# Two ends of a sorted edge list by turns: a new chunk order and one-hots summed on GpSimd in a graph kernel

## The chip, the cores and the metric

One core of a Trainium2 chip runs the whole kernel. The metric is the device time of one execution in microseconds, from the chip's own clock, as the median of several runs. The profile shows one execution: TensorE (PE, with its weight loads as PEld), VectorE (DVE), ScalarE (ACT), GpSimd (POOL), the DMA queues (SPq, ACTq) and the TensorE clock that was granted.

## What is computed

There are N = 12,500 nodes with D = 128 features and E = 200,000 edges. The edges are sorted by their target node `dst`. A target is drawn as 12500·u², so low nodes have very many edges and high nodes few. Each edge has 128 features for layer 1 and 64 for layer 0.

```python
# layer 0
h = relu(layernorm(x))
agg = segment_sum(edge_attr_64 @ W_edge.T, dst)
degree = clip(segment_sum(ones, dst), 1)
out_neigh = (agg / degree) @ W_neigh.T
x = x + concat([h @ W_self.T, out_neigh]) @ W_final.T + b_final
# layer 1
h = relu(layernorm(x))
agg = segment_sum(edge_attr_128, dst)
x = x + relu(concat([h, agg]) @ W1 + b1) @ W2 + b2
```

The two sums over edges and the degrees are nearly all of the memory traffic and most of the matmuls. All of it is float32.

## The kernel before

**Chunks.** The edge list is cut into CH = 128 chunks in order. Chunks 0 to 31 hold 13 units of 128 edges, the others 12, and the last one 7. A chunk is made of 1, 2, 3 or 4 batches (`PARTS`, by quarter of the list). The targets of one batch all lie within a window of WIN = 64 nodes that begins at the batch's first target.

**Sums of a chunk** (`sums`, L447). VectorE builds one-hot rows of every unit in float32 (`one_hots`, L821, one instruction at L817 for a whole chunk, three chunks ahead). TensorE multiplies edge features with them. The array is used as two halves of 64 output rows. L462 and L464 sum the two halves of the 128 features side by side. Then, for two units at a time, L479 sums the 64 features of one unit into one half and those of another into the other, and L482 multiplies a block of ones (bfloat16) with the same one-hots, which gives the degrees. A float32 matmul is issued as two instructions, a bfloat16 one as one. All of it lands in one of three PSUM banks. VectorE adds every batch's window into the running sums `agg` in SBUF at the place that a table of bases gives (`adds`, L842, instruction at L856, one for each batch).

**Order.** The chunks run in the order of the list, so the sums of the nodes become final in the order of the nodes. `agg` is one ring of eight groups of 512 nodes plus a pad of 64 columns, cleared by GpSimd (L357, L383) and folded by VectorE (`fold`, L912). NG = 25 groups of four node tiles (two in the last) are taken when their chunks are through. `READY[g]` says after which chunk. It is 26 for the first group and 119, 122, 125, 127, 128 for the last five, since late chunks hold few edges for each node.

**Ticks.** Every engine's program is one list, written by hand in ticks `t`, one for each chunk and 13 more. Behind the chunk of tick t each engine gets the stages of groups that are due: TensorE's `neigh` at READY (L514, L515), `turn` at +6 (L493), `hidden` at +8 (L526, L527) and `output` at +10 (L534). VectorE has `layer_0` at +1, `stats_2` at +2, `scale_2` at +4 and `result` at +11. GpSimd has `add_b2` at +6 (L378) and `clear` at +9. ScalarE has the rest and the store. A group's own part (layer norm, `turn` and `own_part` at L502, `add_b0` L365 and `add_self` L372 on GpSimd) hangs on no edge and is laid out by `SELF`. It begins at tick 2 and comes every 1.6 ticks up to tick 41.

**Slack between the engines.** Loads run five slots ahead (`load_edges` waits for the sums five chunks back), one-hots three chunks ahead, and `sums(t)` waits for the adds of chunk t-3. `neigh` waits for the adds of the chunk just before.

**Start.** The targets of the list are turned into tables by quarters: `relative` (L805, VectorE), `table` (TensorE, L414), `copy_table` (VectorE). At tick t VectorE has `relative(t + 1)` behind `adds(t)` and `one_hots(t + 3)`, and TensorE has `table(t)` one tick later. `check` (VectorE, tick 6) verifies that every target lies in its window and in the part of the ring that is clear.

Of the kernel before, what the change touches and what calls it, by code (L numbers as in the profile page):

```python
# [14 lines left out]
P = 128  # L15
# [14 lines left out]
RING = 8 * GW  # L30
# [8 lines left out]


def chunk_of(e):
    return int(e // (13 * P)) if e < 32 * 13 * P else int(32 + (e - 32 * 13 * P) // (12 * P))
# [12 lines left out]
def build_gnn(nc, x, dst, edge_attr_128, edge_attr_64, W_self, W_neigh, W_edge, W_final, b_final,  # L55
# [6 lines left out]
    NG = -(-N // GW)  # L62
# [4 lines left out]
    def ready(g):  # L67
        t = GW * (g + 1)
        if t >= N:
            return CH  # L70
        s = (t / N) ** 0.5
        t += 11 * N * s * (s * (1 - s) / E) ** 0.5 + 12
        return min(CH, chunk_of((t / N) ** 0.5 * E) + 1) if t < N else CH

    READY = [ready(g) for g in range(NG)]
    FOLDS = [g for g in range(8, NG, 8)]


    SELF = []
    for g in range(NG):  # L80
        t = max(2 + (8 * g) // 5, SELF[-1] + 1 if g else 0)
        while any(t + 4 == r + 6 or t + 6 == r + 10 for r in READY):
            t += 1
        SELF.append(t)
    TICKS = CH + 13
    assert all(b - a >= 1 for a, b in zip(READY, READY[1:]))
    assert all(SELF[g] + 8 < READY[g] + 1 for g in range(NG))

    def tiles_of(g):
        return min(GN, NT - g * GN)  # L90


    def clear_of(c):
        e = first_edge(c + 1) if c + 1 < CH else E
        return min(NG, int((N * (e / E) ** 2 + WIN + 130) // GW) + 1)

    CLEAR = [max(min(8, c), clear_of(c)) for c in range(CH)]
    for c in range(CH):
        assert CLEAR[c] <= 1 or CLEAR[c] <= min(8, c) or READY[CLEAR[c] - 9] + 9 < c
    ADDED = [0]  # L100
    for c in range(CH):
        ADDED.append(ADDED[-1] + len(batches_of(c)))


    tp_use, row_use = {}, {}
    for t in range(TICKS):
        for g in range(NG):
            if t == READY[g] + 6:
                tp_use["n", g] = len(tp_use)
            if t == READY[g] + 10:  # L110
                row_use["n", g] = len(row_use)
        for g in range(NG):
            if t == SELF[g] + 4:
                tp_use["s", g] = len(tp_use)
            if t == SELF[g] + 6:
                row_use["s", g] = len(row_use)
    assert len(tp_use) == len(row_use) == 2 * NG

    SLOTS = 5
# [3 lines left out]
    X_SEMS = 8  # L123
    WARM_UP = 16
# [6 lines left out]
    PASSES = GW // WIN  # L131

    with ExitStack() as ctx:
# [5 lines left out]

        agg = sb("agg", [P, 3, RING + WIN])  # L140
        x0 = sb("x0", [P, NG, GN, D])
        ring128 = sb("ring128", [P, SLOTS, UNITS, D])
        ring64 = sb("ring64", [P, SLOTS, UNITS, D64])
        onehot = sb("onehot", [P, HOTS, UNITS, WIN])
        rel = sb("rel", [P, 4, UNITS, 32])
        base = sb("base", [1, CH, 4], I16)
        base_pair = base[0:1, :, :].rearrange("p c b -> p (c b)").bitcast(I32)
# [20 lines left out]
        steps_lo = sb("steps_lo", [P, NG])  # L168
        steps_hi = sb("steps_hi", [P, NG])
# [19 lines left out]
        FIRST_SCRATCH = 17  # L189
        flat = x0[:, :, :, :].rearrange("p g t f -> p (g t f)")  # L190
        at = [FIRST_SCRATCH * GW]

        def scratch(cols):
            at[0] += cols
            assert at[0] <= (NG - 2) * GW
            return flat[:, at[0] - cols:at[0]]
# [25 lines left out]
        s_xpad, s_hot, s_mm, s_added, s_zero = (sem(n) for n in ("s_xpad", "s_hot", "s_mm", "s_added", "s_zero"))  # L222
# [26 lines left out]
        def every_group(eng, group):  # L249
            with eng.Fori(0, NG - 1) as g:  # L250
                group(g)
            group(NG - 1)
# [6 lines left out]
        def _(sp):  # L259
# [4 lines left out]
            def load_edges(c):  # L264
                slot, e0, R = c % SLOTS, first_edge(c), run_of(c)
                if c >= SLOTS:
                    sp.wait_ge(s_mm, c - SLOTS + 1)
# [16 lines left out]
            sp.wait_ge(s_store, 16 * (NG + 1))  # L284

            def general():
                sp.dma_start(gen_dst_i, dst.rearrange("(p e) -> p e", p=GP)).then_inc(s_gdst, 16)

                def group(g):
# [7 lines left out]
                    if not isinstance(g, int):  # L297
                        rows = x[bass.ds(g * GW, GW), :].rearrange("(j p) f -> p j f", p=P)
                        sp.dma_start(x0[:, 0, 0:2, :], rows[:, 0:2, :]).then_inc(s_gx, 16)
                        sp.dma_start(x0[:, 0, 2:4, :], rows[:, 2:4, :]).then_inc(s_gx, 16)  # L300
                        sp.wait_ge(s_gstep, g * GSTEPS + GSTEPS + 1)
                        rows = out[bass.ds(g * GW, GW), :].rearrange("(j p) f -> p j f", p=P)
                        sp.dma_start(rows[:, 0:2, :], x0[:, 0, 0:2, :]).then_inc(s_gst, 16)
                        sp.dma_start(rows[:, 2:4, :], x0[:, 0, 2:4, :]).then_inc(s_gst, 16)
                    else:
                        n0 = g * GW
                        sp.dma_start(x0[:, 0, 0, :], x[n0:n0 + P, :]).then_inc(s_gx, 16)
                        sp.dma_start(x0[0:LAST_N, 0, 1, :], x[n0 + P:N, :]).then_inc(s_gx, 16)
                        sp.wait_ge(s_gstep, g * GSTEPS + GSTEPS + 1)
                        sp.dma_start(out[n0:n0 + P, :], x0[:, 0, 0, :]).then_inc(s_gst, 16)  # L310
# [9 lines left out]
        def _(pool):  # L320
# [796 lines left out]
```

## Time and profile before

| | |
|---|---|
| median of 3 runs | 602.6 us (598.23 to 602.62) |
| the profiled execution | 595.72 us, its span 593.9 us |
| PE busy | 539.3 us (91%) |
| PEld busy | 485.2 us (82%) |
| DVE busy | 367.4 us (62%) |
| ACT busy | 150.6 us (25%) |
| POOL busy | 134.7 us (23%) |
| DMA | 169.67 MB, mean 286 GB/s |
| chain that ended last | PE 82%, issue 6%, DVE 5%, ACT 4% |

A busy time is the union of an engine's instructions. PE's idle time over the whole span is 593.9 - 539.3 = 54.6 us. "issue" in a list of waits means that the engine waited for nothing that the profile shows.

### The profile page before, as it was taken

How to read it: one execution, taken by the hardware profiler on the slowest of the kernel's cores; microseconds unless marked ns; L12 is line 12 of the kernel's file. 1: busy time of each engine (PE TensorE's matmuls, PEld its weight loads, DVE VectorE, ACT ScalarE, POOL GpSimd, SP SyncE). 2: the span in 40 equal slices, each digit the busy share in tenths (PEclk: the TensorE clock that was granted, in tenths of full speed). 3: DMA queues.
4: the chain of work that ended last, by engine and by line, in shares of the span. 5: the costliest groups of instructions: out<-in, count | busy, mean ns of one | idle time of the engine just before them, and what ended most of it. 6: DMA issues, size and time to landing. Idle time of an engine off the chain costs nothing.

```text
span 593.9 us, 27741 instructions
## 1 busy us (share of the span) xinstructions
PE 539.3 (91%) x12155; PEld 485.2 (82%) x12155; DVE 367.4 (62%) x1159; ACT 150.6 (25%) x353; POOL 134.7 (23%) x164
## 2 busy tenths in 40 slices
PE   6999889999898989898979889999999989999983
PEld 5998788889787888788869769898988878888852
DVE  3569774566655644454655656666677667676671
ACT  0022344333442451101011211121222122222252
POOL 1233344424423343100001100111111111100020
PEclk9889899999999899998999999999999999999999
DMA  8999899999977787989998988999999989898012
GB/s 281 386 312 374 296 339 335 332 348 321 300 254 265 237 289 250 329 288 343 302 320 286 341 277 297 314 325 308 329 316 333 285 268 304 269 300 253 22 35 65
DMA packets 113236, 169.67 MB, mean 286 GB/s; under 512 B 5486, under 2 KB 84310, under 8 KB 113111
## 3 DMA queue, kind: packets, MB, share of 16 engines
q1 hardware_dynamic: 85843, 154.42, 76.2%
q10 hardware_dynamic: 27268, 13.43, 7.9%
q8 instruction: 98, 1.61, 1.1%
q14 instruction: 27, 0.22, 0.1%
HBM read 161.43 MB, written 6.40 MB: 283 GB/s over the span
## 4 chain that ended last, share of the span: by engine, by line
PE 82%; issue 6%; DVE 5%; ACT 4%; DMA 1%; SPq 1%; DVEq 0%; ACTq 0%
PE ps L462 26%; PE ps L479 17%; PE ps L464 5%; PE ps L502 5%; PE ps L534 4%; PE ps L526 4%; PE ps L514 4%; PE ps L493 4%; PE ps L482 4%; PE ps L515 4%; PE ps L527 3%; ACT hn L681 2%; DMA x<-in_dst_dram 1%; PE ps L406 1%; PE ps L414 1%
## 5 line engine op out<-in xcount | busy, mean ns | idle before, releaser
L462 PEld LDWEIGHTS ps<-onehot,ring 128*64 128x64 f32 x3126 | 197.2, 140 | 28.8 <-issue 24.6
L464 PE MATMUL ps<-onehot,ring 128*64 128x64 f32 x3126 | 215.9, 226 | 3.9 <-issue 3.9
L462 PE MATMUL ps<-onehot,ring 128*64 128x64 f32 x3126 | 215.8, 226 | 2.7 <-issue 2.7
L856 DVE TENSOR_TENSOR agg<-ps,agg 128x128 f32 (+1 forms) x319 | 97.1, 304 | 195.8 <-PE ps L482 138.2
L464 PEld LDWEIGHTS ps<-onehot,ring 128*64 128x64 f32 x3126 | 197.3, 140 | 4.0 <-issue 3.7
L479 PE MATMUL ps<-onehot,ring 128*64 128x64 f32 x3126 | 158.6, 234 | 6.4 <-issue 6.2
L479 PEld LDWEIGHTS ps<-onehot,ring 128*64 128x64 f32 x3126 | 145.4, 139 | 7.9 <-issue 7.7
L482 PE MATMUL ps<-onehot,ones_h 128*64 128x64 bf16 x1563 | 140.0, 194 | 7.8 <-issue 7.8
L817 DVE TENSOR_TENSOR onehot<-iota_win,rel 128x768 f32<-128x768 f32 (+1 forms) x129 | 135.1, 1049 | 0.1
L482 PEld LDWEIGHTS ps<-onehot,ones_h 128*64 128x64 bf16 x1563 | 100.1, 113 | 8.5 <-issue 8.4
L383 POOL MEMSET agg<- 128x1536 f32 x17 | 23.4, 1379 | 182.8 <-PE ps L527 182.8
L709 ACT ACTIVATE h<-x,nmr,rstd 128x128 f32<-128x128 f32 x98 | 40.4, 482 | 81.0 <-DVE nmr L951 79.8
L378 POOL TENSOR_TENSOR x<-x,b_bc 128x512 f32<-128x512 f32 (+1 forms) x25 | 31.4, 1255 | 119.5 <-ACT h L709 119.5
L365 POOL TENSOR_TENSOR x<-x,b_bc 128x512 f32<-128x512 f32 (+1 forms) x25 | 32.3, 1291 | 91.0 <-ACT hn L681 91.0
L681 ACT ACTIVATE hn<-x,nmr,rstd 128x128 f32<-128x128 f32 x98 | 40.4, 485 | 30.7 <-PE ps L493 28.5
L514 PE MATMUL ps<-w_c,agg 128*128 128x129 f32 x196 | 39.6, 283 | 5.4 <-issue 3.4
L372 POOL TENSOR_TENSOR x<-x,own 128x512 f32<-128x512 f32 (+1 forms) x25 | 35.1, 1403 | 17.0 <-ACT own L696 17.0
L515 PE MATMUL ps<-w_c,agg 128*128 128x129 f32 x196 | 37.9, 274 | 0.0
L502 PE MATMUL ps<-w_a,hT 128*128 128x128 f32 x196 | 29.6, 296 | 8.9 <-DVE x L959 5.2
L514 PEld LDWEIGHTS ps<-w_c,agg 128*128 128x128 f32 x196 | 29.9, 190 | 9.3 <-issue 7.5
L724 ACT ACTIVATE hid<-ps,b_col 128x512 f32<-128x512 f32 (+1 forms) x25 | 16.9, 677 | 75.1 <-PE ps L527 45.7
L502 PEld LDWEIGHTS ps<-w_a,hT 128*128 128x128 f32 x196 | 24.8, 198 | 10.8 <-issue 9.4
(109 smaller groups left out, 484.6 us busy)
## 6 DMA issues: line engine op xcount, KB each, us to landing
ring<-in_edge_attr_dram SPq DMA_DIRECT2D x95, 768.0 KB, 5.3
ring<-in_edge_attr_dram SPq DMA_DIRECT2D x96, 384.0 KB, 6.6
ring<-in_edge_attr_dram SPq DMA_DIRECT2D x32, 832.0 KB, 5.8
ring<-in_edge_attr_dram SPq DMA_DIRECT2D x32, 416.0 KB, 7.7
x<-in_x_dram ACTq DMA_DIRECT2D x24, 256.0 KB, 7.5
out_dram<-x ACTq DMA_DIRECT2D x24, 256.0 KB
x<-in_dst_dram SPq DMA_DIRECT2D x1, 384.0 KB
x<-in_dst_dram SPq DMA_DIRECT2D x1, 208.0 KB, 3.3
```

The source lines that it names most:

```text
L372: nc.gpsimd.tensor_tensor(rows, rows, own[:, 0:nt, :], ALU.add).then_inc(s_self, 1)
L462: nc.tensor.matmul(bank[0:H, o:o + WIN], ring128[0:K, slot, u, 0:H], hots, start=u == 0, stop=r == R - 1, skip_group_check=True)
L464: nc.tensor.matmul(bank[H:P, o:o + WIN], ring128[0:K, slot, u, H:D], hots, start=u == 0, stop=r == R - 1, skip_group_check=True)
L479: nc.tensor.matmul(bank[feats, o:o + WIN], ring64[0:K, slot, u, :], onehot[0:K, hot, u, :], start=False, stop=True, skip_group_check=True)
L482: last = nc.tensor.matmul(bank[count, o:o + WIN], ones_h[0:K, :], halves[0:K, u, :, 1], start=False, stop=True, skip_group_check=True)
L502: last = nc.tensor.matmul(ps_row[:, j * D:(j + 1) * D], hT[:, j * P:(j + 1) * P], w_a[:], start=True, stop=True)
L514: nc.tensor.matmul(ps_nb[:, j // 2, j % 2, :], agg[:, 1, nodes], w_c[:, 0, :], start=True, stop=False)
L515: last = nc.tensor.matmul(ps_nb[:, j // 2, j % 2, :], agg[:, 2, nodes], w_c[:, 1, :], start=False, stop=True)
L681: last = nc.scalar.activation(hn[:, j, :], x0[:, g, j, :], ACT.Relu, bias=nmr1[:, u, j:j + 1], scale=rstd1[:, u, j:j + 1])
L709: last = nc.scalar.activation(h2[:, j, :], x0[:, g, j, :], ACT.Relu, bias=nmr2[:, u, j:j + 1], scale=rstd2[:, u, j:j + 1])
L817: nc.vector.tensor_tensor(onehot[0:K, c % HOTS, u0:u1, :], iota_win[0:K, :].unsqueeze(1).to_broadcast([K, n, WIN]), rel[0:K, c // 32, a:a ...
L856: nc.vector.tensor_tensor(here, ps[:, c % BANKS, o:o + w * WIN].rearrange("p (a n) -> p a n", a=w), here, ALU.add).then_inc(s_added, 1)
```

## The change

1. **Chunk order.** `ORDER` takes chunks 8 to 13 first. Then it takes one from the high end (127, 126, ... down to 71) and one from the low end (14, 15, ... up to 70) by turns. Chunks 0 to 7, whose targets all lie in node tile 0, come last.
2. **Two rings.** `agg` holds tile 0 (128 columns), a ring of four groups for the low side and a ring of four groups for the high side, each with a pad. The groups are now tile 0 alone, then 512 nodes each, and one tile at the end (NG = 26). They are taken in the order `SEQ` at the ticks `TAKE`: 9, 15, 21, 27, 31, 36, 39, 45, 51, 54, 57, 63, 70, 71, 77, 84, 85, 93, 96, 101, 108, 109, 118, 119, 120, 128. The last one is tile 0. Group 8 gets sums from both rings and needs twice the `agg` matmuls.
3. **Degrees.** GpSimd adds the one-hots of the units of a batch (`hot_sums`, two to three adds of 128 to 384 columns a chunk, output bfloat16). TensorE then does 2 to 4 count matmuls a chunk at its end instead of one for each unit, behind a wait for GpSimd.
4. **Own parts** are laid out at least nine ticks ahead of `TAKE` and two ticks apart, over ticks 0 to 119, not 2 to 41.
5. **Start.** `table` moves one tick up, and `relative` and `copy_table` move ahead of `one_hots`. `check` is cut into three parts at ticks 6, 8 and 10. The base table takes five small instructions instead of two.
6. ScalarE's list puts `turned` and `hidden` ahead of the norms.

```diff
+    for t in range(CH - DENSE):
+        if t < LEAD_IN or (t - LEAD_IN) % 2:
+            ORDER.append(low)
+            low += 1
+        else:
+            ORDER.append(high)
+            high -= 1
+    ORDER += range(DENSE)
...
+    for q in range(NG - 1, -1, -1):
+        t = min(TAKE[q] - 9, SELF[0] - 2 if SELF else CH)
...
+            def hot_sums(at):
+                c = ORDER[at]
+                pool.wait_ge(s_hot, at + 1)
+                if at >= HOTS:
+                    pool.wait_ge(s_mm, at - HOTS + 1)
+                if at:
+                    pool.wait_ge(s_hotsum, HOT_SUMS[at])
...
+                elif c < 32:
+                    pool.wait_ge(s_hotsum, add(t[:, 0:6, :], h[:, 0:6, :], h[:, 6:12, :]))
+                    pool.wait_ge(s_hotsum, add(s[:, 0:2, :], t[:, 0:2, :], t[:, 2:4, :]))
+                    add(s[:, 0:2, :], s[:, 0:2, :], t[:, 4:6, :])
...
+                else:
+                    pool.wait_ge(s_hotsum, add(t[:, 0:4, :], b[:, :, 0, :], b[:, :, 1, :]))
+                    add(s[:, 0:4, :], t[:, 0:4, :], b[:, :, 2, :])
...
             for t in range(TICKS):
+                if t + AHEAD - 1 < CH:
+                    hot_sums(t + AHEAD - 1)
...
                     for (u, K, o), feats in here:
                         nc.tensor.matmul(bank[feats, o:o + WIN], ring64[0:K, slot, u, :], onehot[0:K, hot, u, :],
                                          start=False, stop=True, skip_group_check=True)
-                    for (u, K, o), _, count in here:
-                        last = nc.tensor.matmul(bank[count, o:o + WIN], ones_h[0:K, :], halves[0:K, u, :, 1],
-                                                start=False, stop=True, skip_group_check=True)
+                sums_of_hots, single = counts_of(c)
+                for u, h, i, K in single:
+                    nc.tensor.matmul(bank[h * H:h * H + H, places[i][h]:places[i][h] + WIN], ones_h[0:K, :], halves[0:K, u, :, 1],
+                                     start=False, stop=True, skip_group_check=True)
+                pe.wait_ge(s_hotsum, HOT_SUMS[t + 1])
+                for k, (h, i, K) in enumerate(sums_of_hots):
+                    last = nc.tensor.matmul(bank[h * H:h * H + H, places[i][h]:places[i][h] + WIN], ones_h[0:K, :], hot_sum[0:K, hot, k, :],
+                                            start=False, stop=True, skip_group_check=True)
                 last.then_inc(s_mm, 1)
...
              for t in range(TICKS):
                 if t < CH:
                     sums(t)
-                if 1 <= t <= 3:
-                    table(t)
-                if 2 <= t <= 4:
-                    weights(t - 2)
+                if t < 3:
+                    table(ZONES[t + 1])
+                if 1 <= t <= 3:
+                    weights(t - 1)
...
                      adds(t)
+                    if t < 3:
+                        relative(ZONES[t + 1])
+                    if 1 <= t <= 3:
+                        copy_table(ZONES[t])
                     if t + AHEAD < CH:
                         one_hots(t + AHEAD)
```

## Rows read from the trace of the kernel before

**Rows 1.** Stretches: us, then busy us (count) per engine, clock, DMA share, GB/s.

```profile
0.00:42.00 42.00, 35.98 (x548) 33.89 (x550) 22.83 (x45) 3.20 (x5) 9.30 (x69) 0.88 0.94 329
42.00:240.00 198.00, 176.99 (x4227) 163.96 (x4224) 123.84 (x404) 75.86 (x191) 75.28 (x56) 0.97 0.88 303
240.00:564.00 324.00, 308.13 (x7282) 274.63 (x7283) 207.65 (x658) 60.40 (x134) 45.57 (x35) 0.99 0.89 291
564.00:594.00 30.00, 18.16 (x115) 12.72 (x113) 13.12 (x52) 11.16 (x26) 4.53 (x4) 0.98 0.17 50
sum 594.00, PE 539.26 PEld 485.20 DVE 367.44 ACT 150.61 POOL 134.68; mean PE 134.82 PEld 121.30 DVE 91.86 ACT 37.65 POOL 33.67
```

**Rows 2.** Waits of TensorE, whole span: us in total, times, longest us.

```profile
PE ps L482 <- issue: 7.8, 7, 1.9
...
PE ps L502 <- DVE x L959: 5.2, 2, 2.6
...
PE ps L493 <- ACT hT L689: 3.8, 6, 1.8
...
PE ps L502 <- ACT own L696: 3.7, 3, 2.5
...
PE ps L462 <- issue: 2.7, 5, 0.8
```

**Rows 3.** Waits of VectorE over the whole span.

```profile
DVE agg L856 <- DVE agg L856: 37.4, 191, 0.5
DVE agg L856 <- issue: 20.0, 32, 3.4
```

**Rows 4.** The stretch 450:550 alone, columns as in rows 1.

```profile
450.00:550.00 100.00, 97.18 (x2106) 84.60 (x2102) 70.04 (x235) 22.30 (x49) 15.76 (x12) 1.00 0.90 283
```

**Rows 5.** Waits of VectorE in the same stretch.

```profile
DVE agg L856 <- PE ps L482: 9.0, 8, 1.7
```

**Rows 6.** Timeline of TensorE in chunk 64: start, duration (us), engine, line.

```profile
300.42 0.22 PE L462 MATMUL ps<-onehot,ring 128*64 128x64 f32 x1
...
301.59 0.22 PE L462 MATMUL ps<-onehot,ring 128*64 128x64 f32 x1
...
301.82 0.20 PE L482 MATMUL ps<-onehot,ones_h 128*64 128x64 bf16 x2
...
302.69 0.20 PE L482 MATMUL ps<-onehot,ones_h 128*64 128x64 bf16 x2
```

**Rows 7.** Groups by line: the matmuls of the degrees; busy us, mean ns.

```profile
L482 PE MATMUL ps<-onehot,ones_h 128*64 128x64 bf16 x1563 | 140.0, 194 | 7.8 <-issue 7.8
```

**Rows 8.** Timeline of TensorE behind the last chunk: a group's next stages.

```profile
564.72 1.12 PE L526 MATMUL ps<-agg,w1b 128*128 128x512 f32 x2
```

**Rows 9.** Timeline of VectorE while the tables are made, near the start.

```profile
25.54 1.75 DVE L805 TENSOR_TENSOR x<-x,firsts 32x1536 f32<-32x1536 int32 x1
```

**Rows 10.** Groups by line, shapes apart: GpSimd's add at two widths.

```profile
L378 POOL TENSOR_TENSOR x<-x,b_bc 128x512 f32<-128x512 f32 x24 | 30.7, 1277 | 118.7 <-ACT h L709 118.7
...
L372 POOL TENSOR_TENSOR x<-x,own 128x256 f32<-128x256 f32 x1 | 0.7, 730 | 8.2 <-ACT own L696 8.2
```

**Rows 11.** Timeline: a GpSimd add and a VectorE one-hot meet.

```profile
104.17 1.27 POOL L372 TENSOR_TENSOR x<-x,own 128x512 f32<-128x512 f32 x1
...
104.43 1.90 DVE L817 TENSOR_TENSOR onehot<-iota_win,rel 128x832 f32<-128x832 f32 x1
```

**Rows 12.** Groups by line: VectorE's one-hots, GpSimd's three adds of a group.

```profile
L817 DVE TENSOR_TENSOR onehot<-iota_win,rel 128x768 f32<-128x768 f32 (+1 forms) x129 | 135.1, 1049 | 0.1
...
L372 POOL TENSOR_TENSOR x<-x,own 128x512 f32<-128x512 f32 (+1 forms) x25 | 35.1, 1403 | 17.0 <-ACT own L696 17.0
...
L365 POOL TENSOR_TENSOR x<-x,b_bc 128x512 f32<-128x512 f32 (+1 forms) x25 | 32.3, 1291 | 91.0 <-ACT hn L681 91.0
...
L378 POOL TENSOR_TENSOR x<-x,b_bc 128x512 f32<-128x512 f32 (+1 forms) x25 | 31.4, 1255 | 119.5 <-ACT h L709 119.5
```

**Rows 13.** Timeline of ScalarE's queue: the last store.

```profile
589.57 0.44 ACTq L655 DMA_DIRECT2D out_dram<-x  x1
```

More of the change, by code:

```diff
@@ L85, in build_gnn @@
-    TICKS = CH + 13
[L86 to L99, printed above, removed]
@@ new lines, in begin_of, with end_of, tiles_of, tile_of @@
+    def begin_of(g):
+        return P + (g - 1) * GW if g else 0
+    def end_of(g):
+        return min(N, begin_of(g + 1))
+    def tiles_of(g):
+        return -(-(end_of(g) - begin_of(g)) // P)
+    def tile_of(g):
+        return begin_of(g) // P
+    def place(edge, sign):
+        s = edge / E
+        return N * s * s + sign * (11 * N * s * (s * (1 - s) / E) ** 0.5 + 12)
+    reach = []
+    for c, side in zip(ORDER, SIDE):
+        lo, hi = place(first_edge(c), -1), place(first_edge(c + 1) if c < CH - 1 else E, 1) + WIN
+        reach.append([0] if side == "dense" else [g for g in range(NG) if lo < end_of(g) and hi >= begin_of(g)])
@@ new lines, in build_gnn, with cleared, bounds @@
+    for q, g in enumerate(SEQ):
+        for at, other in ((P, g + 4 if g and g in LOWER else 0), (UPPER_AT, g - 4 if g in UPPER else 0)):
+            if other in (LOWER if at == P else UPPER) and other:
+                a = at + (g - 1) % 4 * GW
+                CLEARS.append((TAKE[q] + 9, a, a + GW))
+    CLEARS.sort(key=lambda x: x[0])
+    def cleared(t):
+        return sum(1 for k, _, _ in CLEARS if k + 2 <= t)
+    def bounds(t):
+        if SIDE[t] == "dense":
+            return 0, P
+        done = CLEARS[:cleared(t)]
+        free = {g for g in range(NG) if TAKE[TURN[g]] > t}
+        if SIDE[t] == "bottom":
+            lo = min(g for g in free if g) if 1 not in free else 0
+            hi = lo
+            while hi + 1 in LOWER and hi + 1 in free and (hi < 4 or TAKE[TURN[hi - 3]] + 11 <= t):
+                hi += 1
+            end = begin_of(hi + 1)
+            for k, a, b in CLEARS[:8]:
+                if k + 2 > t and a < UPPER_AT:
+                    end = min(end, a)
+            return begin_of(lo), end
+        hi = max(free)
+        lo = hi
+        while lo - 1 in UPPER and lo - 1 in free and (lo - 1 > NG - 5 or TAKE[TURN[lo + 3]] + 11 <= t):
+            lo -= 1
+        return begin_of(lo), N + WIN if hi == NG - 1 else begin_of(hi + 1)
@@ new lines, in build_gnn, with changes @@
+    for t in range(CH):
+        lo, hi = bounds(t)
+        assert SIDE[t] == "dense" or lo <= max(0, place(first_edge(ORDER[t]), -1)), (t, ORDER[t], lo, hi)
+        assert hi >= min(N, place(first_edge(ORDER[t] + 1) if ORDER[t] < CH - 1 else E, 1)) + (0 if SIDE[t] == "dense" else WIN), (t, ORDER[t], lo, hi)
+        assert SIDE[t] != "top" or t >= 6
+    def changes(k):
+        values = [bounds(AT[c])[k] for c in range(CH)]
+        return [(c, values[c] - (values[c - 1] if c else 0)) for c in range(CH) if c == 0 or values[c] != values[c - 1]]
@@ L123, in build_gnn @@
     X_SEMS = 8
+    X_LEAD = 6
     WARM_UP = 16
@@ new lines, in store, with inputs @@
+            def store(q):
+                g = SEQ[q]
+                n0, n1, j0 = begin_of(g), end_of(g), tile_of(g)
+                act.wait_ge(s_rowc, row_use["n", q] + 1)
+                if g == NG - 1:
+                    act.dma_start(out[n0:n1, :], x0[0:n1 - n0, j0, :]).then_inc(s_store, 16)
+                else:
+                    act.dma_start(out[n0:n1, :].rearrange("(j p) f -> p j f", p=P), x0[:, j0:j0 + tiles_of(g), :]).then_inc(s_store, 16)
+            def inputs(t):
+                for q in range(NG):
+                    if t == SELF[q] - X_LEAD:
+                        load_x(q)
@@ L657, in _ @@
+            for t in range(-X_LEAD, 0):
+                inputs(t)
             act.wait_ge(s_const, N_CONST)
```

805 lines of the change are left out of this document (436 added, 369 removed).

## The prediction, made before the changed kernel was run

> **What bounds the kernel now.** I read the stretches first. From 42 to 564 us TensorE is busy 485.1 of 522 us, while VectorE, the next, is busy 331.5 [rows 1]. So TensorE's list sets the pace, and a part pays as it takes instructions off it or closes its idle time. That idle time is 6.0 us at the start, 21.0 and 15.9 in the two middle stretches and 11.8 behind the last chunk, 54.7 in all [rows 1].
>
> The waits say what the middle 36.9 us are. Five rows "<- issue", of which the first and the last are shown, sum to 24.0 us (7.8, 6.2, 3.9, 3.4, 2.7). Nothing is awaited there, and most lie inside a chunk. The waits of `own_part` and `turn` for VectorE's result and for ScalarE's two copies are 5.2, 3.8 and 3.7, together 12.7 us [rows 2]. They belong to the own parts, which come every 1.6 ticks up to tick 41. No load is in the list.
>
> VectorE's real load is more than its busy time. Between dependent adds it stands 37.4 us, and 20.0 us on "issue" [rows 3]. So it is engaged 367.4 + 37.4 + 20.0 = 425 us, or 3.32 us for each of the 128 ticks. How full it may be is shown by 450:550, where every chunk has four batches. TensorE was busy 97.2 us of 100 there [rows 4], and VectorE waited for it only 9.0 [rows 5], so VectorE was 91% engaged. The three banks carry that.
>
> **Degrees.** In a chunk, twenty steps of L462, two instructions each with L464, take 301.59 - 300.42 = 1.17 us, 29 ns an instruction. Five rounds of four L479 and two L482 take 302.69 - 301.82 = 0.87 us, or 174 ns a round [rows 6]. Four at 29 are 117, which leaves 57 for two counts, 28.5 ns each. The mean of 194 ns [rows 7] is the latency and no price. Counts before: 1563 [rows 7]. After: 32 chunks by 3, 32 by 2, 63 by 4 and 3 in the last, 415. So 1148 go, 32.7 us. Bounds: 0, if each only fills a hole between float32 steps, and 45 us, if what stays is hidden too. I take 32.7, which is near the row's own round.
>
> **Group 8 twice.** Four tiles get two more `agg` matmuls and `hidden` gets one more over 512 columns, 1.12 us [rows 8]. With the tiles it is 2.5 us (between 1.1 and 4). TensorE's busy time becomes 539.3 - 32.7 + 2.5 = 509.1 us. Nothing else changes its instructions.
>
> **Start.** `table` now comes right behind the sums of ticks 0, 1 and 2, and waits for `relative`, which VectorE begins only behind the add of that same chunk. Before, a tick lay between. `relative` takes 1.75 us [rows 9]. With the hop and the add ahead of it TensorE stands about 2.7 us, three times, 8 us. Bounds 0 (VectorE was ahead) and 10. Idle at the start becomes 14 us. What is late next is chunk 3, and nothing else. The five base instructions run before the first chunk is through.
>
> **Own parts.** Spread over 120 ticks, ScalarE's copies stop being late, and 12.7 us go. The check in three parts helps in the same place.
>
> **GpSimd.** An add of 512 columns takes 1277 ns, one of 256 takes 730 [rows 10]. The line through them is 2.14 ns a column and 183 ns, so 384 columns take 1.00 us and 128 take 0.46. A chunk's adds take 1.92 us (first two quarters), 1.64 and 1.46, in all 222 us. With its 134.7 [rows 1] that is 2.79 us a tick, and some 0.3 for its own hand-overs. Bfloat16 outputs and short strided inputs aren't in the trace. Bounds are the line and 1.5 times the line. I take the line, since the rows on it are of the same operation. The sums of chunk t + 2 stand first in tick t, ahead of `add_b2`, so a late ScalarE costs nothing until GpSimd lags two ticks. TensorE waits for them behind the last count. Queued behind that wait are `neigh`, `hidden` and the rest of the tick, and the slot's next load and VectorE's adds hang on the same semaphore.
>
> The Trainium skill ("GPSIMD Engine Reference", Engine selection) says that elementwise adds of two inputs belong on VectorE, since GpSimd is about twice as slow, 4497 ns for 2048 columns. By its figure per column (estimate 2.2 ns) the adds would take nearly what the line gives. It speaks against the change only if GpSimd or VectorE is full.
>
> **The lock.** A one-hot that began 0.26 us into a GpSimd add took 1.90 us and ended 0.89 us behind the add's [rows 11]. A one-hot alone takes 0.95 to 1.02 us, so it stood until the add was over.  GpSimd's three adds of a group are busy 98.8 us, 17% of the span, and the one-hots average 1049 ns, which is 12 us above 129 of them alone [rows 12]. The 50 small scaling instructions of the norms also read two SBUF inputs; estimate 50 x 0.17 x 0.87 = 7 us. So the adds cost VectorE 19 us now. After, adds are busy 222 + 98.8 = 321 us, 3.3 times as much, so VectorE stands some 64 us, 0.50 a tick. Its load is 3.32 - 0.15 + 0.50 = 3.67 us a tick. TensorE needs (509.1 - 15.6 at the start) / 128 = 3.85 and 0.19 of holes, 4.04 us. That is 91%, the share that cost nothing before. But three lists are now coupled in every chunk, so I put 12 us of new waits (0 to 25) in the place of the 12.7.
>
> The Trainium skill ("SBUF — State Buffer", Who interferes with whom) calls this an exclusive lock for the whole instruction between GpSimd and a VectorE instruction with two SBUF inputs. The trace agrees: 1.90 us in place of 1.02.
>
> **Tail.** Before, 11.8 us of the last 30 were idle, and the last store's issue lay 4.3 us ahead of the end [rows 1, 13]. After, one tile passes all stages alone, but three groups' `output` run beside it. I take 10 us idle (8 to 12). The tail is shorter, near 16 us for 29, but most of the difference is work moved forward, not removed.
>
> **Loads.** 303 GB/s at a share of 0.88 and 291 at 0.89 [rows 1] give 327 to 344 at full share, so 169.7 MB need 493 to 519 us, below the sum here. They stay hidden.
>
> **The sum.** 509.1 + 14 (start) + 24 (holes) + 12 (new waits) + 10 (tail) = 569 us, against 593.9: 25 us less. The profiled execution, 595.7 us, lies 7 below the median of 602.6. I carry the difference over: 602.6 - 25 = 578 us.
>
> **The rivals.**
> - *Nothing gets in the way* (0.20). 450:550 speaks for it. Waits 2 us, holes 20 with fewer instructions: 509 + 14 + 20 + 2 + 9.5 = 554.5, 39 less: 563 us.
> - *The lock makes VectorE the bound* (0.13). If each one-hot stands 0.73 us and each of 50 scaling instructions 0.87, the load is 3.17 + 0.73 + 0.34 = 4.24 a tick, 0.2 over TensorE. Over 120 ticks that is 24 us in place of my 12: 509 + 14 + 24 + 24 + 10 = 581, so 590 us. For it speaks the pair of [rows 11], against it that GpSimd starts its adds when the one-hot ends.
> - *GpSimd is the bound, and the kernel slower* (0.07). If adds cost 1.5 times the line and one per tick also waits out a one-hot, a tick is (333 + 134.7)/128 + 0.3 + 0.95 = 4.9 us, 1.05 over the bare 3.85. 120 ticks give 126 us of idle in place of holes and waits: 509 + 14 + 126 + 10 = 659, 668 us. It turns slower from (594 - 509 - 24)/120 = 0.51 us over the 3.85, which is adds at 1.2 times the line.
> - *Half the counts were free* (0.09). Removing them gives 16 us: 594 us.
> - *Transfers bound* (0.03). Rates would have to fall under 311 GB/s over the whole run; the time would be about 600 us.
>
> **Chances.** My forecast has 0.48, with a range of its own of 568 to 588. Faster by over 1%, what a measurement of this kernel can tell from no change, means under 596.6. It holds the forecast, the first rival and about half of the second and fourth: 0.80. Within 1%: the rest of these, 0.11. Slower 0.09. The range goes from the first rival's low side, 558, to 600, past the cases at 590 and 594. It leaves out the slow rival and the fringes.
>
> **What would show it.** L482 x415 and PE busy near 509 us for the counts. L414 waiting for DVE L805 by some 8 us for the start. `own_part` rows gone from the waits. L817's mean up to 1.3 to 1.5 us for the lock; above 1.7 the second rival is right. PE waiting for POOL `hot_sum` by under 5 us, and GpSimd's add of 384 columns near 1.0 us; 1.2 or more would make me wrong on the slow side.

## The result, and the profile after

The changed kernel took 629.3 us (median of 4 runs, 622.1 to 632.9). The kernel before took 602.6. The ratio is 1.044 (95% interval 1.033 to 1.054). On another chip, beside the experiments, it was 1.053 (1.047 to 1.058). The forecast was 578 us, with a range of 558 to 600. So the change made the kernel slower, and the forecast, which gave "slower" a chance of 0.09, is wrong on the sign. Ratios leave out executions more than 1.5% above the fastest of their kernel: one of the four here, and two of e2's four, its profiled one among them.

The stretches of the changed kernel, columns as in [rows 1]; the last one ends with the span, 626.1 us:

```profile
0.00:42.00 42.00, 28.93 (x367) 27.31 (x367) 22.39 (x33) 3.23 (x4) 19.03 (x59) 0.88 0.74 261
42.00:240.00 198.00, 174.13 (x4038) 158.23 (x4039) 137.45 (x411) 49.16 (x117) 127.53 (x187) 0.96 0.91 310
240.00:564.00 324.00, 281.27 (x5874) 249.96 (x5870) 209.21 (x661) 91.92 (x209) 201.26 (x263) 0.94 0.84 283
564.00:626.00 62.00, 45.26 (x760) 38.66 (x760) 20.98 (x71) 11.84 (x29) 14.88 (x21) 0.86 0.26 87
sum 626.00, PE 529.59 PEld 474.17 DVE 390.03 ACT 156.15 POOL 362.70; mean PE 132.40 PEld 118.54 DVE 97.51 ACT 39.04 POOL 90.67
```

Counted by its chunk sums, the changed kernel is behind at 42 us (78 instructions of L622 for 130 of L462) and ahead at 240 us (1262 for 1218). The loss lies behind that. From 240 to 564 us TensorE stands 42.7 us, where it stood 15.9. Its mean clock over the span is 0.932 and was 0.979. TensorE is busy 529.6 us in place of the forecast's 509.1 and idle 96.5 in place of 60.

The waits of TensorE over the whole span (us, times, longest), the lines that answer [rows 2]:

```profile
PE ps L669 <- DVE x L1137: 26.6, 7, 5.9
PE ps L684 <- DVE x L1108: 10.3, 5, 4.9
PE ps L705 <- DVE x L1137: 9.7, 3, 3.6
PE ps L574 <- DVE x L978: 8.1, 3, 3.3
PE ps L684 <- issue: 8.1, 3, 4.3
```

L669 is `own_part`, L684 `neigh`, L705 `output`, L574 `table`. L1137 is VectorE's `result`, L1108 its `layer_0`. Fifteen waits for these two cost 46.6 us. In the kernel before, the two waits of `own_part` for `result` were 5.2 us [rows 2]. The longest of the fifteen, at tick 74, as VectorE and TensorE show it in the timeline (start, us):

```profile
349.58 0.95 DVE L997 TENSOR_TENSOR onehot<-iota_win,rel 128x768 f32<-128x768 f32 x1
350.45 0.86 DVE L1117 BATCH_NORM_STATS2 bn<-x 128x6 f32<-128x128 f32 x4
...
351.82 0.45 DVE L1081 SCALAR_TENSOR_TENSOR nmr<-mv,rstd 128x4 f32<-128x4 f32 x1
352.79 0.29 DVE L1026 TENSOR_TENSOR agg<-ps,agg 128x128 f32 x1 [0.52 <-issue]
353.27 0.29 DVE L1026 TENSOR_TENSOR agg<-ps,agg 128x128 f32 x1 [0.19 <-DVE agg L1026]
353.76 0.36 DVE L1026 TENSOR_TENSOR agg<-ps,agg 128x192 f32 x1 [0.20 <-DVE agg L1026]
354.04 0.95 DVE L997 TENSOR_TENSOR onehot<-iota_win,rel 128x768 f32<-128x768 f32 x1
354.91 0.68 DVE L1137 TENSOR_TENSOR x<-ps,x 128x512 f32<-128x512 f32 x1
...
355.73 2.05 PE L669 MATMUL ps<-w_a,hT 128*128 128x128 f32 x8 [5.86 <-DVE x L1137]
```

`own_part` and `output` share one PSUM bank, `ps_row`. In tick 73 TensorE ran `output`. In tick 74 it has the chunk's sums and then `own_part`, which needs the bank back. The bank is free when VectorE has run `result`. That stands in VectorE's tick 74 behind three adds (1.3 us with their gaps) and a one-hot. The adds in turn can start only when TensorE has ended the sums just before its own wait, and when VectorE is through with tick 73. Here TensorE stands from 349.87 us, and VectorE has the one-hot and the norm work of tick 73 until 352.27. So TensorE stands for what VectorE still owes of the tick before, and for what lies ahead of `result` in this one. The other fourteen waits are 0.3 to 4.9 us long. In the plan `own_part` is at SELF + 6 and `result` at TAKE + 11. By the two lists they fall on the same tick at 42, 68, 74 and 82, and TensorE waited at all four. The own part comes one tick behind at 33, 48, 51, 66, 89, 105 and 113, and TensorE waited at 33, 89 and 113. The `TAKE` list has neighbours (70 and 71, 84 and 85, 108 and 109, 118 to 120). There `neigh` of a group waits for `layer_0` of the group taken one tick earlier (L684, 5 times), and its `output` waits for that group's `result` (L705, 3).

### The profile page after: what moved, and what is told of

The parts are those of the page before. It is cut to its first block, busy times and chain, and to the rows that moved or that the text cites. A ratio compares the mean times of both kernels' runs of the same rounds, so it can differ in the third digit from the quotient of the medians.

```text
span 626.1 us, 26025 instructions
## 1 busy us (share of the span) xinstructions
PE 529.6 (85%) x11029; PEld 474.2 (76%) x11029; DVE 390.0 (62%) x1173; ACT 156.2 (25%) x359; POOL 362.7 (58%) x529
## 4 chain that ended last, share of the span: by engine, by line
PE 59%; DVE 25%; issue 7%; DVEq 3%; POOL 2%; ACT 2%; DMA 1%; SPq 0%; ACTq 0%; POOLq 0%
PE ps L622 20%; PE ps L640 10%; PE ps L684 9%; DVE onehot L997 8%; DVE agg L1026 6%; PE ps L669 4%; PE ps L697 3%; PE ps L660 3%; PE ps L624 3%; PE ps L698 3%; PE ps L705 3%; DVE x L1108 2%; DVEq L1026 2%; DVE x L1137 2%; DVE bn L1117 2%
## 5 line engine op out<-in xcount | busy, mean ns | idle before, releaser
L513 POOL TENSOR_TENSOR hot_part<-onehot 128x384 bf16<-128x384 f32 (+2 forms) x128 | 111.7, 873 | 224.4 <-DVE onehot L997 217.9
L622 PEld LDWEIGHTS ps<-onehot,ring 128*64 128x64 f32 x3126 | 203.8, 145 | 27.4 <-issue 22.9
L624 PE MATMUL ps<-onehot,ring 128*64 128x64 f32 x3126 | 221.5, 231 | 2.7 <-issue 2.7
L622 PE MATMUL ps<-onehot,ring 128*64 128x64 f32 x3126 | 221.3, 231 | 0.7 <-issue 0.7
L997 DVE TENSOR_TENSOR onehot<-iota_win,rel 128x768 f32<-128x768 f32 (+2 forms) x128 | 137.2, 1073 | 0.2
L640 PE MATMUL ps<-onehot,ring 128*64 128x64 f32 x3126 | 119.4, 225 | 5.6 <-issue 5.4
L684 PE MATMUL ps<-w_c,agg 128*128 128x129 f32 x408 | 60.7, 310 | 22.3 <-DVE x L1108 10.3
L684 PEld LDWEIGHTS ps<-w_c,agg 128*128 128x128 f32 x408 | 56.3, 220 | 28.1 <-issue 23.3
L669 PE MATMUL ps<-w_a,hT 128*128 128x128 f32 x196 | 32.3, 314 | 26.6 <-DVE x L1137 26.6
L669 PEld LDWEIGHTS ps<-w_a,hT 128*128 128x128 f32 x196 | 27.4, 216 | 27.8 <-issue 27.2
L513 POOL TENSOR_TENSOR hot_sum<-hot_part 128x128 bf16<-128x128 bf16 x96 | 44.1, 460 | 7.5
L491 POOL TENSOR_TENSOR x<-x,b_bc 128x512 f32<-128x512 f32 (+1 forms) x26 | 32.9, 1268 | 14.2 <-ACT h L888 14.2
L705 PE MATMUL ps<-w,hid 128*128 128x128 f32 x196 | 30.6, 302 | 11.0 <-DVE x L1137 9.7
L513 POOL TENSOR_TENSOR hot_sum<-hot_sum,hot_part 128x128 bf16<-128x128 bf16 x64 | 35.0, 547 | 5.0
L705 PEld LDWEIGHTS ps<-w,hid 128*128 128x128 f32 x196 | 25.8, 204 | 13.3 <-issue 10.5
L499 POOL MEMSET agg<- 128x1536 f32 (+2 forms) x26 | 35.8, 1378 | 0.0
```

The source lines that it names most:

```text
L499: nc.gpsimd.memset(agg[:, :, a:b], 0.0).then_inc(s_zero, 1)
L513: nc.gpsimd.tensor_tensor(out, a, b, ALU.add).then_inc(s_hotsum, 1)
L622: nc.tensor.matmul(bank[0:H, o:o + WIN], ring128[0:K, slot, u, 0:H], hots, start=u == 0, stop=r == R - 1, skip_group_check=True)
L624: nc.tensor.matmul(bank[H:P, o:o + WIN], ring128[0:K, slot, u, H:D], hots, start=u == 0, stop=r == R - 1, skip_group_check=True)
L640: nc.tensor.matmul(bank[feats, o:o + WIN], ring64[0:K, slot, u, :], onehot[0:K, hot, u, :], start=False, stop=True, skip_group_check=True)
L669: last = nc.tensor.matmul(ps_row[:, j * D:(j + 1) * D], hT[:, j * P:(j + 1) * P], w_a[:], start=True, stop=True)
```

## The experiments

Ratios are to the kernel before, timed in the same job on the same chip. "Clock lost" is one minus the mean granted clock, times the span.

| | edit | median us | ratio (95%) | PE busy | PE idle | clock |
|---|---|---|---|---|---|---|
| before (first profile) | | 602.6 | 1 | 539.3 | 54.7 | 0.979 |
| after (first profile) | | 629.3 | 1.044 (1.033 to 1.054) | 529.6 | 96.5 | 0.932 |
| e4 | after, without sums on GpSimd | 646.0 | 1.081 (1.066 to 1.095) | 557.0 | 87.5 | 0.945 |
| e3 | sums on GpSimd alone | 594.9 | 0.995 (0.988 to 1.002) | 510.5 | 77.6 | 0.967 |
| e1 | after, ticks kept apart | 595.7 | 0.998 (0.992 to 1.003) | 520.3 | 73.1 | 0.951 |
| e2 | after, `result` and `layer_0` early | 574.1 | 0.953 (0.937 to 0.970) | 518.2 | 58.2 | 0.951 |
| e8 | after, start put back | 618.0 | 1.043 (1.029 to 1.056) | 524.3 | 88.5 | 0.940 |
| e10 | e2 without sums on GpSimd | 597.7 | 1.000 (0.994 to 1.006) | 543.9 | 52.2 | 0.967 |
| e11 | after, six waits filled with matmuls | 623.7 | 1.051 (1.037 to 1.064) | 547.3 | 72.4 | 0.960 |
| e9 | old order, sums, early, own parts over 8..104 | 580.9 | 0.976 (0.967 to 0.985) | 513.4 | 68.0 | 0.958 |
| e12 | after again | 628.7 | 1.053 (1.047 to 1.058) | 532.2 | 97.0 | 0.923 |
| e13 | e2 again | 574.5 | 0.963 (0.955 to 0.971) | 512.1 | 58.8 | 0.968 |
| e14 | e2 with start put back | 561.7 | 0.942 (0.936 to 0.947) | 510.6 | 48.7 | 0.972 |
| e15 | old order, sums, early, own parts over 1..58 | 580.3 | 0.972 (0.967 to 0.977) | 512.1 | 68.5 | 0.970 |

There were three jobs after the first profiles: e1 to e4, e8 to e11, and e12 to e15. The kernel before had medians of 599.6, 597.9 and 596.5 us in them. Differences of a few us between jobs are not read.

**Which half of the change costs.**

e3: the kernel before with `hot_sums`, `counts_of` and the 415 count matmuls.

> The kernel before with GpSimd's sums of one-hots and the 415 count matmuls alone, order, plan and start as before. Theory A: TensorE loses 32.7 us of matmuls and little else changes: about 572 against 602.6. Theory B: GpSimd's adds delay VectorE's one-hots and norms, 603 or more.

e4: the changed kernel without them:

```diff
-            for t in range(AHEAD - 1):
-                hot_sums(t)
...
-                pe.wait_ge(s_hotsum, HOT_SUMS[t + 1])
+                    for (u, K, o), _, count in here:
+                        last = nc.tensor.matmul(bank[count, o:o + WIN], ones_h[0:K, :], halves[0:K, u, :, 1], ...)
```

> The changed kernel with the degrees counted on TensorE for each unit as before and no sums on GpSimd. Theory A: the waits for VectorE's x stay above 30 us and 33 us of matmuls come back: 640 to 660. Theory B: with GpSimd's 228 us of adds gone the waits go too: 610 or less.

The rest of the change (the new order with its plan of own parts, its start and ScalarE's list) is 8% slower by itself, and its waits for L1127 and L1098 (`result` and `layer_0` there) are those of the changed kernel, 24.1, 10.0 and 9.3 us. So GpSimd's work isn't what makes `result` late. The sums alone take 28.8 us off TensorE's busy time (539.3 to 510.5), but the kernel gains 0.5% and is the same within its interval, between the two forecasts of 572 and 603. Where its gain went is in TensorE's waits in e3 (us, times, longest):

```profile
PE ps L563 <- ACT hT L759: 13.5, 9, 3.0
PE ps L572 <- ACT own L766: 8.4, 5, 4.5
...
PE ps L572 <- DVE x L1029: 6.1, 2, 3.3
```

L563 is `turn`, L572 `own_part`. The own parts of the old plan come every 1.6 ticks. With TensorE quicker through its chunks, the hand-overs to ScalarE and VectorE in between are late: 28.0 us of waits on these rows, where [rows 2] has 12.7.

**The waits for x, taken away in two ways.**

e1 keeps the ticks apart:

```diff
-        TAKE.append(max(READY[g], TAKE[-1] + 1 if TAKE else 0))
+        TAKE.append(max(READY[g], TAKE[-1] + 2 if TAKE else 0))
...
-        while any(t + 4 == r + 6 or t + 6 == r + 10 for r in TAKE):
+        while any(t + 4 == r + 6 or t + 6 in (r + 10, r + 11, r + 12) for r in TAKE):
```

> The changed kernel with another plan and nothing else: groups are taken at least two ticks apart, and no own part falls on the tick of a group's result or the one behind it. Theory A (the plan puts a TensorE stage in the same tick as the VectorE stage that it needs; each such meeting costs 3 to 6 us and then a slow clock): the three waits of TensorE for VectorE's x (46.6 us in the changed kernel) fall under 12 us, the time at half clock goes from 88 us towards 40, and the median from 629 to about 575. Theory B (GpSimd's sums and the shared lock slow VectorE down, so that TensorE waits wherever it stands): other waits take their place, time above 615.

e2 leaves the plan and moves VectorE's two stages to the head of their tick:

```diff
             for t in range(TICKS):
+                for q in range(NG):
+                    if t == TAKE[q] + 1:
+                        layer_0(q)
+                    if t == TAKE[q] + 11:
+                        result(q)
                 if t < CH:
                     adds(t)
...
                 for q in range(NG):
-                    if t == TAKE[q] + 1:
-                        layer_0(q)
...
-                    if t == TAKE[q] + 11:
-                        result(q)
```

> The changed kernel, its plan untouched, but VectorE does layer_0 and result of a tick ahead of that tick's adds and one-hots instead of behind them. Theory A: the same three waits fall under 12 us by the other way, median about 575 to 585. Theory B: VectorE has as much to do as before, time above 615.

Both confirm the cause, at 1.044 against 0.998 and 0.953. With e1 the waits for L1137 and L1108 fall from 46.6 to 4.7 us, as forecast, but its 595.7 us are 20 above the forecast of 575. L660, `turn`, waits 9.5 us for ScalarE's `hT`, the rows "issue" are 22.9 us for 16.9, and the clock is 0.951. So e1 shows where the waits come from, and e2 what they are worth. With e2, repeated as e13, they are short. The waits of TensorE in e13:

```profile
PE ps L640 <- issue: 7.6, 7, 1.8
PE ps L574 <- DVE x L978: 7.3, 3, 2.5
...
PE ps L669 <- DVE x L1137: 3.6, 4, 2.0
```

Every group of matmuls is the same in both. Only the place of two calls on another engine differs, and it is worth 54 us on one chip (628.7 to 574.5, e12 and e13), where the waits for these two lines fall from 47.0 to 4.5 us.

> The changed kernel once more, beside the next three on the same chip, so that their differences can be read without the chips' own. Theory (the cause is VectorE's place of result and layer_0, 15 of whose ticks collide with an own part, an output or a neigh): ratio to the kernel before 1.03 to 1.055, as measured. Rival (the 4% is a chip's own): under 1.02.

> VectorE's layer_0 and result stand ahead of the adds and one-hots of their tick, all else as changed. Theory: TensorE's waits for x fall from some 45 us to under 8, and the ratio to the kernel before is 0.95 to 0.965, 8% under the changed kernel on the same chip. Rival (most of the loss is the new order's and the sums' own): at least 1.0.

**What the sums are worth once nothing waits.** e10 is e4 with the edit of e2.

> The run e2_early with the degrees counted on TensorE for each unit and no sums on GpSimd. It prices the sums apart from the meetings. If the sums are as good as free (the lock hardly costs), 33 us more than e2_early: about 605. If the lock and the hand-over to GpSimd cost VectorE's and TensorE's time, less than 15 us more: under 590.

TensorE is busy 543.9 us in e10 and 512.1 in e13, 31.8 us less, where 32.7 were forecast. The times say 0.963 and 0.953 against 1.000, some 22 to 28 us, between the two forecasts for e10. The new order with the edit of e2 and without the sums is level with the kernel before (1.000), so in that form, with the start's cost still in it, the order gives nothing.

**Where the rest of the loss is: the clock.** In e11 six of the own parts that wait have 24 spare matmuls ahead of the wait, into a bank that nobody reads then. Their products are thrown away, nothing is left out.

```diff
+                if SELF[q] + 6 in (42, 68, 74, 82, 89, 113):
+                    pe.wait_ge(s_added, ADDED[SELF[q] + 5])
+                    for _ in range(24):
+                        nc.tensor.matmul(ps[:, (SELF[q] + 7) % BANKS, 0:P], ones_f[:], ident[:], ...)
                 if row_use["s", q]:
                     pe.wait_ge(s_rowc, row_use["s", q])
```

> The changed kernel with 24 spare matmuls (ones times identity, 48 instructions, some 2.8 us) put ahead of own_part's wait for VectorE in the six ticks 42, 68, 74, 82, 89 and 113, into the PSUM bank of the next chunk; their results are thrown away. The wait is just as long, only filled. If the slow clock is what follows TensorE's idle time, the falls behind these six waits go, some 25 us less at half clock, and the time falls 5 to 12 us below the changed kernel's. If the clock has another cause, the time stays or rises by up to 5 us, with the same 86 us at half clock.

The stretches around tick 42, the wait, 2 us behind it and the 4 us after, first in the changed kernel, then in e11 (columns as in [rows 1], the clock is the number ahead of the DMA share):

```profile
203.00:208.70 5.70, 0.92 (x34) 0.83 (x31) 4.49 (x17) 0.30 (x1) 3.27 (x4) 1.00 1.07 369
208.70:210.70 2.00, 1.99 (x11) 2.00 (x12) 1.02 (x8) 0.00 (x0) 1.19 (x3) 0.64 0.87 281
210.70:214.70 4.00, 4.00 (x102) 3.67 (x103) 0.29 (x1) 1.27 (x3) 0.00 (x0) 0.76 0.02 5
```

```profile
203.00:208.40 5.40, 5.40 (x49) 5.40 (x50) 4.19 (x18) 0.30 (x1) 3.55 (x5) 1.00 1.05 364
208.40:210.40 2.00, 2.00 (x35) 1.83 (x35) 0.57 (x5) 0.57 (x2) 0.82 (x2) 1.00 0.69 224
210.40:214.40 4.00, 4.00 (x137) 3.96 (x132) 1.89 (x5) 0.70 (x3) 0.40 (x1) 1.00 0.24 38
```

With the engine busy through the wait the clock stays at 2.4 GHz behind it. With the wait left idle it drops to its other level, 1.2 GHz, for a part of the next 6 us, which hold 113 instructions for 172. The eight instructions of `own_part` take 1.56 us behind the idle wait and 1.06 behind the filled one. In the 4 us behind the six waits the mean clock is 0.57, 0.50, 0.53, 1.00, 0.50 and 0.57 in the changed kernel, and 1.00 six times in e11. The Trainium skill ("TensorE: Matmul & The Clock Gate", What's actually happening) says that the gate has these two rates and goes to the lower one after idleness; the two fences agree. Over the span e11 loses 24.8 us of clock and the changed kernel 42.6. Without the 33.8 us of spare matmuls TensorE is busy 513.5 us in e11, for 529.6. But the spare matmuls took 5.6 us at each place for the 2.8 expected, more than five of the six waits. The 5 to 12 us that were forecast can't be seen: its time isn't told apart from the changed kernel's, 1.051 (1.037 to 1.064) beside 1.044 and 1.053. So e11 shows what the clock does, and not that a filler pays.

A price for it comes from the changed kernel and e13, whose TensorE lists are the same. Busy time differs by 17.5 us (529.6 and 512.1), clock lost by 24.3 (42.6 and 18.3). Between e12 and e13, on one chip, it is some 20 us of busy time and 30 of clock lost.

**The start.** e8 and e14 put `table`, `relative`, `copy_table` and the weights back to their old ticks, without and with the edit of e2:

```diff
-                if t < 3:
-                    table(ZONES[t + 1])
                 if 1 <= t <= 3:
-                    weights(t - 1)
+                    table(ZONES[t])
+                if 2 <= t <= 4:
+                    weights(t - 2)
...
+                    if 2 <= t <= 4:
+                        copy_table(ZONES[t - 1])
+                    if t + AHEAD < CH:
+                        one_hots(t + AHEAD)
                     if t < 3:
                         relative(ZONES[t + 1])
-                    if 1 <= t <= 3:
-                        copy_table(ZONES[t])
-                    if t + AHEAD < CH:
-                        one_hots(t + AHEAD)
```

> The changed kernel with tables, weights, relative and copy_table back on their old ticks, one behind for TensorE. If the start was sized right, the 8.1 us of TensorE's waits for DVE x L978 go and with them some of the slow clock of the first 60 us: 10 to 14 us less than the changed kernel, about 616 to 620. If VectorE only has the same work later, less than 4 us.

> The kernel of the run before it, and table, relative and copy_table back in the places of the kernel before. Theory: the wait of table for relative, 8 us, goes, and nothing takes its place, as the next chunks' loads are there: 6 to 8 us under the run before it, ratio 0.94 to 0.955. Rival (the lead at the start is eaten again by the 14 us of other waits or by transfers): within 2 us of the run before it.

e8 has the time that was forecast for it, 618.0 us, but it can't be told from the changed kernel, since they ran in different jobs (1.043 beside 1.044 and 1.053). e14 can, beside e13: 561.7 against 574.5 us, 12.8 less, more than the 6 to 8 expected. The stretches of the three waits, first e14, then e13:

```profile
17.00:30.00 13.00, 12.11 (x260) 11.73 (x260) 9.63 (x13) 0.29 (x1) 11.03 (x13) 0.87 1.01 383
30.00:46.00 16.00, 15.02 (x346) 13.87 (x344) 8.54 (x15) 1.99 (x7) 15.34 (x76) 1.00 0.79 249
```

```profile
17.00:30.00 13.00, 9.72 (x189) 9.26 (x188) 6.61 (x12) 0.00 (x0) 8.78 (x12) 0.87 0.86 328
30.00:46.00 16.00, 11.98 (x157) 11.13 (x159) 8.05 (x10) 2.38 (x5) 6.93 (x66) 0.68 0.36 121
```

The three waits are 7.3 us in e13 and 0.9 in e14. In the second stretch of e13 the clock is 0.68, and it holds less than half of the instructions. Up to the same place of TensorE's list, first e14, then e13:

```profile
0.00:49.30 49.30, 42.88 (x756) 40.02 (x758) 29.21 (x49) 3.83 (x10) 34.36 (x107) 0.93 0.90 306
```

```profile
0.00:58.30 58.30, 46.12 (x757) 42.87 (x759) 30.33 (x48) 5.12 (x11) 30.97 (x106) 0.85 0.72 253
```

Here e13 is 9 us behind, 3.2 of it busy time. At the end of the two profiled executions it is 11.5 us behind, 10.1 of it idle and 1.5 busy. Of the idle time 6.4 us are the three waits and 3.4 are "issue". So the edit is worth more than its waits, but little of the rest is shown to be the clock. e14 is the fastest kernel of the study, 5.8% under the kernel before.

**Is the new order worth its trouble?** e9 and e15 are e3 with VectorE's two stages early and the own parts spread, in the old order of the chunks.

> The kernel before, its chunk order kept, with GpSimd's sums of one-hots, own parts spread over ticks 8 to 104 and kept off the ticks of results, and VectorE's layer_0 and result ahead of the adds. In e3_counts_only TensorE waited 22 us for ScalarE's copies of the own parts and 6 for VectorE's result; if these ate the gain of the counts, they go here and the time is about 565 to 572. If the old chunk order itself sets a bound (tail, four adds a chunk in a row at the end), above 585.

> The kernel before with GpSimd's sums and 415 counts, layer_0 and result ahead of the adds, and the own parts spread over ticks 1 to 58, kept off a group's output and result. It leaves out the new order of the chunks and the second ring. Theory (the new order itself gives little, since a tick's stages are the same work wherever they stand): PE busy 511, the waits of own_part under 6, tail 11.8 idle as before: ratio 0.955 to 0.975. Rival (spreading the groups over the whole run is what pays): the new order is better by 10 us or more, ratio here 0.975 to 0.99, with the difference in the last 30 us and in falls of the clock.

The own parts in e15:

```diff
-        t = max(2 + (8 * g) // 5, SELF[-1] + 1 if g else 0)
-        while any(t + 4 == r + 6 or t + 6 == r + 10 for r in READY):
+        t = max(1 + (9 * g) // 4, SELF[-1] + 1 if g else 0)
+        while any(t + 4 == r + 6 or t + 6 in (r + 9, r + 10, r + 11) for r in READY):
```

e9 took 580.9 us, above the 565 to 572 of its forecast. A new row stands at the head of its waits:

```profile
PE ps L605 <- ACT own L767: 19.5, 8, 4.1
```

L605 is `output`. I kept own parts off the tick of `output` and the one behind it, but not off the one ahead. There the bank is handed over by ScalarE's copy within a tick, and TensorE stands. e15 keeps off that tick too, and the row is gone. But other waits take its place: 0.972 beside 0.976, and TensorE's idle time is 68.5 us for 68.0. The waits of e15 for ScalarE:

```profile
PE ps L563 <- ACT hT L759: 9.3, 8, 2.4
...
PE ps L572 <- ACT own L766: 7.0, 4, 2.8
```

e15 is at 0.972, e14 at 0.942 on the same chip: the new order, with its plan of own parts, `check` in parts and ScalarE's list, is worth 18.6 us here, more than the 10 of e15's rival, though e15 itself lies in the range of its theory. TensorE's busy time is the same (512.1 and 510.6), and the difference is idle time, 68.5 for 48.7. Of it 12.7 us are in the two rows above (16.3 in e15, while e14 has 3.6 for `hT` and none for `own`), 8 are "issue" (28.4 and 20.0 over all such rows). Little of it is in the last 30 us, where e15's rival had it: TensorE is idle 11.9 us there in e15 and 10.5 in e14. But e15's own parts are not a best plan, and a better one might take away more of these waits. What the order is worth against the best plan of the old one stays open. Why "issue" is larger wasn't traced. Nor was the edit of e2 tried by itself on the kernel before, where TensorE's waits for `result` and `layer_0` are 8.0 us.

## Why the prediction was wrong

**The step that failed** is "Spread over 120 ticks, ScalarE's copies stop being late, and 12.7 us go", with its "12 us of new waits (0 to 25)" in their place. The first half held: the wait for ScalarE's `own` is gone in the changed kernel. The second didn't. I took the spread as a change of density and never laid the list of `SELF` + 6 over the list of `TAKE` + 11, nor looked for neighbours in `TAKE`. Both lists stand in the change. A meeting costs what VectorE has ahead of `result` in its tick: from the rows above three adds, 1.3 us with their gaps, the one-hot's 0.95 and `result`'s 0.68, 2.9 us, and what it still owes of the tick before. As an estimate, fifteen meetings at 2.9 are 44 us; measured were 46.6, against a bound of 25 for all new waits. That the two sums are close is partly luck, since the single waits run from 0.3 to 5.9 us and the five for `layer_0` have another list ahead of them. The old plan had two at 5.2 us [rows 2], and that row named the price. I read it as a row that would disappear.

**The second error** is that idle time was priced at its own length. By the first profiles 20.5 us of the miss are busy time (529.6 for 509.1), with the same instructions. e13, without the waits, is busy 512.1. The forecast's sum took TensorE's clock as it was and had no term for it.

**Held against e13**, the kernel with that one fault taken out, the terms of the sum were these:

| term | forecast | changed kernel | e13 |
|---|---|---|---|
| PE busy | 509.1 | 529.6 | 512.1 |
| all idle | 60 | 96.5 | 58.8 |
| of it: `table`, three times | 8 | 8.1 | 7.3 |
| holes, "issue" | 24 | 16.9 | 23.4 |
| waits for `result` and `layer_0` | in the 12 | 46.6 | 4.5 |
| last 30 us | 10 | 10.1 | 10.5 |
| span | 569 | 626.1 | 570.8 |

(The rows "issue" and "waits for" are sums over all rows of TensorE's waits with that releaser.) The sum was right for a kernel that wasn't the changed one.

**Degrees.** Right: 31.8 us of busy time between e10 and e13, 32.7 forecast; L649 has 382 of the 415 count matmuls. e3 shows that they pay only when nothing else is waiting.

**Start.** The wait was right (8.1 us for 8). Its worth wasn't: 12.8 us between the medians of e13 and e14. In the profiles 6.4 us of the 11.5 are the waits, 3.4 are "issue" and 1.5 busy time.

**GpSimd.** Right. The rows of its adds in the changed kernel, shapes apart, answer [rows 10]:

```profile
L513 POOL TENSOR_TENSOR hot_part<-onehot 128x384 bf16<-128x384 f32 x64 | 65.5, 1024 | 141.8 <-DVE onehot L997 136.3 <-PE ps L649 5.1 <-POOL hot_sum L513 0.2
...
L513 POOL TENSOR_TENSOR hot_sum<-hot_part 128x128 bf16<-128x128 bf16 x96 | 44.1, 460 | 7.5
```

The line gave 1.00 and 0.46 us. No wait of TensorE for `hot_sum` is in its list. The rival "GpSimd is the bound", the only one on the slow side, had the right sign by another mechanism.

**The lock.** The forecast put VectorE's standing at 64 us after 19, 45 more. For the one-hots it was wrong. The mean of those of 768 columns is 1019 ns in the kernel before, 1074 in the changed kernel and 1120 in e13, for a forecast of 1.3 to 1.5 us. 217.9 us of GpSimd's idle time end on a one-hot, so GpSimd's chain begins when the one-hot ends and is mostly over before the next. For the small scaling instructions of the norms it was right. Their rows, and the one-hot's, in e13, with GpSimd's sums:

```profile
L997 DVE TENSOR_TENSOR onehot<-iota_win,rel 128x768 f32<-128x768 f32 x95 | 106.4, 1120 | 0.0
...
L1129 DVE SCALAR_TENSOR_TENSOR nmr<-mv,rstd 128x4 f32<-128x4 f32 x24 | 17.0, 710 | 0.8
L1081 DVE SCALAR_TENSOR_TENSOR nmr<-mv,rstd 128x4 f32<-128x4 f32 x24 | 16.5, 687 | 0.8
```

and in e10, without them:

```profile
L987 DVE TENSOR_TENSOR onehot<-iota_win,rel 128x768 f32<-128x768 f32 x95 | 102.2, 1076 | 0.0
...
L1119 DVE SCALAR_TENSOR_TENSOR nmr<-mv,rstd 128x4 f32<-128x4 f32 x24 | 6.7, 281 | 0.8
L1071 DVE SCALAR_TENSOR_TENSOR nmr<-mv,rstd 128x4 f32<-128x4 f32 x24 | 4.7, 198 | 0.8
```

The 48 scaling instructions take 33.5 us for 11.4, and the 95 one-hots 4.2 us more, 26 us of VectorE in all, for the 45 forecast. e13 hides most of it: TensorE's idle time is 58.8 us with the sums and 52.2 without. One of the meetings in its timeline:

```profile
332.60 0.95 DVE L997 TENSOR_TENSOR onehot<-iota_win,rel 128x768 f32<-128x768 f32 x1
333.46 0.17 DVE L1127 RECIPROCAL rstd<-std 128x4 f32<-128x4 f32 x1
333.62 1.00 POOL L513 TENSOR_TENSOR hot_part<-onehot 128x384 bf16<-128x384 f32 x1 [2.92 <-DVE onehot L997]
333.67 0.97 DVE L1129 SCALAR_TENSOR_TENSOR nmr<-mv,rstd 128x4 f32<-128x4 f32 x1
```

GpSimd's add began when the one-hot was over, the scaling instruction 0.05 us later. It took 0.97 us and ended 0.02 us behind the add.

**Order of the lists.** "But three lists are now coupled in every chunk" was the right worry at the wrong pair: VectorE's order within a tick sets it, since e13 has the same work on VectorE and 4.5 us of these waits.

## What to carry to other kernels

When stages are moved on a tick plan, lay the ticks of every pair that shares a buffer over each other, and the same for neighbours in the list. A hand-over within one tick costs all that stands ahead of it on the releasing engine, with what that engine still owes of the tick before. A release that a tighter engine waits for belongs at the head of its tick, ahead of work that has slack: here that was worth 54 us, more than any part of the change. Price a stall of TensorE above its length, because the clock can be lower behind it: between e12 and e13, 42.5 us of waits went with 54 us of time and some 20 us of TensorE's busy time.

## What was not expected of the hardware

- Five of six waits of 3 to 6 us were followed by a clock at 1.2 GHz for part of the next few us (0.64 and 0.76 in the fence of tick 42), and spare matmuls in the wait held it at 1.00 at all six. Between two kernels with the same TensorE list, 24.3 us of clock lost went with 17.5 us of busy time.
- A GpSimd chain that is started by the end of a VectorE instruction with two SBUF inputs hardly meets the next of its kind (1120 ns for 1076), but does meet the small instructions right behind it (198 ns became 687). The Trainium skill ("SBUF — State Buffer", Who interferes with whom) says that VectorE's instructions with two SBUF inputs and GpSimd's reads exclude each other, and that the order of issue decides who blocks. The trace agrees: in the timeline above the add began 0.05 us ahead of the scaling instruction, and that one took 0.97 us.
